# A fused graph network: 92 of 391 edge chunks sorted by source in four classes, ranked in the edge stage, with one-hots shared with ScalarE

## What is computed

```
sums, counts = segment_sum(edge_attr, dst), segment_sum(1, dst)
h0 = concat(x, sums / max(counts, 1), global_feats) @ W.T
x  = layernorm(x + softplus(h0) - log 2)
h  = relu(ln(x @ W1 + b1) * g1 + bt1)
w  = sigmoid(relu(concat(h[src], h[dst]) @ We1 + be1) @ We2 + be2)
aggr = segment_sum(w * h[src], dst)
gate = sigmoid(concat(h, aggr) @ Wg + bg)
x  = layernorm(x + ln(gate * aggr + (1 - gate) * h) * g2 + bt2)
```

## Time and profile before

| | us |
|---|---|
| median of 3 runs (2357.36 to 2359.33) | 2358.75 |
| profiled execution, whole time | 2364.05 |
| its span, first to last instruction | 2362.3 |
| busy in the span: TensorE | 1540.2 |
| VectorE | 1695.0 |
| ScalarE | 582.4 |
| GpSimd | 1452.0 |
| mean granted clock of TensorE | 0.691 of full |

### The profile page before, as it was taken

How to read it: one execution, slowest core, us unless ns; L and a number is a source line. 1 busy time by engine, 2 the same in 40 slices (tenths; PEclk the granted TensorE clock), 3 DMA queues, 4 the chain that set the end, 5 groups by cost and what they waited for, 6 DMA issues and landing times.

```text
span 2362.3 us, 38568 instructions
## 1 busy us (share of the span) xinstructions
PE 1540.2 (65%) x11768; PEld 1351.2 (57%) x11769; DVE 1695.0 (72%) x6954; ACT 582.4 (25%) x1425; POOL 1452.0 (61%) x1465
## 2 busy tenths in 40 slices
PE   5999978973445655665546666667666766665670
PEld 4777867753444544544446666656666655655540
DVE  6666756747988665665557777777778887787767
ACT  0212114640001998888000000000000000000025
POOL 2000001437777777777777777777777777777766
PEclk9999996775555566556556666776767667777675
DMA  7889990145444444444454555555555555555401
GB/s 273 309 304 318 357 345 12 59 150 169 128 132 132 137 135 137 131 130 135 151 163 133 152 157 165 165 163 164 165 159 166 157 168 155 156 163 163 125 22 55
DMA packets 224719, 387.44 MB, mean 164 GB/s; under 512 B 78295, under 2 KB 118264, under 8 KB 224383
## 3 DMA queue, kind: packets, MB, share of 16 engines
q1 hardware_dynamic: 155671, 200.17, 25.7%
q0 software_dynamic: 64704, 176.77, 25.4%
q10 hardware_dynamic: 4136, 8.03, 1.0%
HBM read 369.81 MB, written 15.02 MB: 163 GB/s over the span
## 4 chain that ended last, share of the span: by engine, by line
POOL 38%; PE 27%; issue 19%; DVE 10%; DVEq 2%; DMA 1%; ACT 1%; ACTq 1%; SPq 0%; POOLq 0%
POOL x_rows L717 23%; POOL ring L717 15%; PE bank L402 9%; PE bank L1123 4%; PE bank L449 3%; PE bank L1064 3%; PE bank L409 3%; DVE bank L438 2%; PE bank L429 1%; PE bank L1036 1%; DVEq L1562 1%; DVE sums L1453 1%; PE bank L1015 1%; PE bank L1073 1%; DVE stats L1360 1%
## 5 line engine op out<-in xcount | busy, mean ns | idle before, releaser
L717 POOL DMA_INDIRECT x_rows<-src_table,lane_src x816 | 801.4, 982 | 271.2 <-issue 247.7
L717 POOL DMA_INDIRECT ring<-src_table,lane_src x532 | 522.5, 982 | 162.1 <-issue 161.5
L1138 PE MATMUL bank<-sums 128*128 128x128 f32 x588 | 210.0, 458 | 354.1 <-issue 346.2
L438 DVE SCALAR_TENSOR_TENSOR bank<-bank,we_all 128x128 f32<-128x128 f32 x1642 | 420.5, 324 | 13.0 <-issue 0.4
L1138 PEld LDWEIGHTS bank<-sums 128*128 128x128 f32 x588 | 148.5, 310 | 363.0 <-issue 363.0
L453 DVE TENSOR_TENSOR sums<-sums,bank 128x128 f32 (+1 forms) x728 | 178.2, 245 | 190.3 <-issue 127.5
L686 POOL TENSOR_TENSOR ring<-ring,x_rows 128x512 f32<-128x512 f32 (+1 forms) x13 | 15.7, 1204 | 408.3 <-DVE ring L1350 408.3
L919 ACT ACTIVATE sums<-sums,be_all 128x3 f32<-128x3 f32 x98 | 29.1, 297 | 952.1 <-DVE bank L438 952.1
L449 PE MATMUL bank<-weighted,x_rows 128*128 128x40 f32 x1632 | 254.2, 326 | 2.2 <-DVE sums L453 2.1
L449 PEld LDWEIGHTS bank<-weighted,x_rows 128*128 128x128 f32 x1632 | 253.3, 244 | 2.9 <-issue 2.9
L438 DVE DVE_READ_ACCUMULATOR bank<-bank,we_all 128x1 f32 x1642 | 228.1, 139 | 0.4
(11 more groups left out here) (216 smaller groups left out, 2753.3 us busy)
## 6 DMA issues: line engine op xcount, KB each, us to landing
ring<-in_edge_attr SPq DMA_DIRECT2D x195, 512.0 KB, 5.4
ring<-rel_table SPq DMA_DIRECT2D x84, 512.0 KB, 4.7
x_rows<-src_table,lane_src POOLq DMA_INDIRECT x816
ring<-cell_table SPq DMA_DIRECT2D x33, 384.0 KB, 5.0
ring<-dst_table SPq DMA_DIRECT2D x337, 32.0 KB
ring<-src_table,lane_src POOLq DMA_INDIRECT x532
sums<-src_table SPq DMA_DIRECT2D x49, 128.0 KB, 2.1
src_table<-ring SPq DMA_DIRECT2D x12, 512.0 KB, 3.7
```

Of the source, the lines that this page charges most:

```text
L438: last = eng.scalar_tensor_tensor(hid[:, j, :], hid[:, j, :], 0.0, wide["we2"][:, :], ALU.max, ALU.mult, accum_out=out[:, j:j + 1])
L717: eng.indirect_dma_start(gathered(c)[:, j, :], None, src_table, bass.IndirectOffsetOnAxis(ap=lane_src[:, t:t + 1], axis=0)).then_inc(gathe ...
L1138: eng.matmul(o, src_hot[:, u % 2, k * P:(k + 1) * P], block_rows[:, b % B_SLOTS, 0:P], start=True, stop=False, skip_group_check=True)
```

## The change

The sizes. A class is (first chunk, chunks, cells of 128 for each block). A class has a base row of its own (its first start), so that its destinations lie in 128 nodes from there.

```diff
-SORTED = 54
-CAP = 6
-HALF = CAP // 2
+CLASSES = ((0, 39, 4), (39, 18, 2), (57, 18, 2), (75, 17, 2))
+SORTED = 92
+COLS = 4
...
-    V_SLOTS, G_SLOTS, Q_SLOTS, Q_BATCH = 8, 10, 16, 4
+    V_SLOTS, G_SLOTS, Q_SLOTS, Q_BATCH = 8, 8, 16, 4
...
+        SORT_STEPS = [10] + [3] * (n_classes - 1)
+        SORT_AT = [1]
+        for k in range(1, n_classes):
+            SORT_AT.append(SORT_AT[-1] + sort_len(k - 1) + 5)
...
+        RIDE_AT = CELLS_OUT[0] + 4
+        FOLD_LAG = 2
         def ride(u):
+            return RIDE_AT + u * (n_steps - 1 - FOLD_LAG - RIDE_AT) // (n_riders - 1)
```

**Edge stage.** ScalarE makes the one-hots of pairs 7, 11, ..., 195 (48), three pairs ahead:

```diff
+            def scalar_hot(q):
...
+                for k, c in enumerate(chunks):
+                    for j in range(J):
+                        eng.activation(hots[:, k, j, :], iota1[:, :], ACT.Abs, bias=lane_dst[:, c, j:j + 1], scale=-1.0)
+                eng.drain()
...
+                eng.activation(flat, flat, ACT.Relu, bias=ones[:, 0:1], scale=-1.0).then_inc(done("scalar_hot"), 1)
...
                 eng.activation(pair_rows[0:r, q % 2, :], bank[q % 2][0:r, 0:P], ACT.Copy).then_inc(done("pair_rows"), 1)
+                if q + HOT_PAIRS in scalar_hots:
+                    scalar_hot(q + HOT_PAIRS)
```

On VectorE `hot(q)` does a drain and a semaphore for these pairs, and at set pairs a part of the ranking: `classes_prepared` (pair 3), `couples` (4), a `scan` over 372 for each of 25 couples of blocks (pairs 12 to 14, 30 to 32, ...), `before_`, `check_totals` (166), `kept` (170), `ranked` in five parts (172 to 176). A couple is two blocks; the odd one counts in 2048s. On GpSimd, nine parts of three couples each:

```diff
+            def rank_in(i):
+                n = len(part_couples(i))
+                for k, b in enumerate(part_couples(i)):
+                    eng.tensor_scalar(in_couple[:, i % 2, k, :], couple, float(b), None, ALU.is_equal)
+                eng.drain()
+                eng.tensor_tensor(in_couple[:, i % 2, 0:n, :], in_couple[:, i % 2, 0:n, :],
+                                  parity.unsqueeze(1).to_broadcast([P, n, rank_tokens]), ALU.mult).then_inc(done("rank"), 1)
...
+            def rank_pick(i):
...
+                eng.tensor_tensor(r[:, :, 0:rank_tokens0], r[:, :, 0:rank_tokens0], first_, ALU.add)
+                for k in range(1, n_classes):
...
+                    eng.tensor_tensor(r[:, :, some], r[:, :, some], before[:, i % 2, 0:n, k:k + 1].to_broadcast([P, n, rank_span]), ALU.add)
+                eng.drain()
+                eng.tensor_tensor(r, r, in_couple[:, i % 2, 0:n, :], ALU.mult)
+                for k in range(n):
+                    eng.drain()
+                    last = eng.tensor_tensor(pos[:, :], pos[:, :], r[:, k, :], ALU.add)
```

**Gather stage.** The ranking leaves it. `sort_start` goes to step 0. VectorE's one-hots of the sort carry the value, two a token, and ScalarE makes one column one-hot a token for both (Abs, Relu, width 196 or 98):

```diff
+            def sort_rows(q):
                 for k, t in enumerate(sort_tokens(q)):
+                    for v, value in enumerate((src_low, sorted_dst)):
+                        eng.tensor_scalar(sort_hot(q)[0][:, k, v, :], iota_r, row_of[:, t:t + 1], value[:, t:t + 1], ALU.is_equal, ALU.mult)
```

ScalarE takes over the cell one-hots, the source placement and the copy of the sums; TensorE accumulates in PSUM and folds each rider; the hidden part of a rider has one bank and goes last in TensorE's step:

```diff
             for q in range(n_steps):
                 edge_weight(q)
+                if q - 2 in riders:
+                    sums_out(q - 2)
+                if q in riders:
+                    place_sources(q)
+                if q + 3 in riders:
+                    cell_hots(q + 3)
+                if q + 3 in sort_class:
+                    sort_columns(q + 3)
...
-            run_stages(n_steps, [(1, hidden_mm), (4, wsum)])
+            run_stages(n_steps, [(1, hidden_mm), (4, wsum), (1, rider_mm)])
```

More of the change, by code:

```diff
@@ L680, in residual @@
+            need(eng, "hot", KEYS_AT)
+            rank_in(0)
+            rank_in(1)
+            for i in range(n_parts):
+                rank_totals(i)
+                rank_pick(i)
+                if i + 2 < n_parts:
+                    rank_in(i + 2)
             def residual(g):
@@ new lines, in cell_hots @@
+            def cell_hots(q):
+                u = riders[q]
+                need(eng, "rider_hidden", u - 2)
+                eng.wait_ge(rider_in[u % U_SLOTS], 32 * (u // U_SLOTS + 1))
+                n = rider_cols(u) * P
+                hots = (src_hot[:, u % 2, 0:n], dst_hot[:, u % 2, 0:n])
+                for v, hot_ in enumerate(hots):
+                    eng.activation(hot_, cell_wide[:, u % U_SLOTS, v, 0:n], ACT.Abs, bias=iota_col[:, 0:1])
+                eng.drain()
+                for hot_ in hots:
+                    last = eng.activation(hot_, hot_, ACT.Relu, bias=ones[:, 0:1], scale=-1.0)
+                last.then_inc(done("cell_hot"), 1)
@@ new lines, in place_sources @@
+            def place_sources(q):
+                u = riders[q]
+                need(eng, "wsum", q - 2)
+                n = rider_cols(u)
+                at_ = rider_cells(u).start
+                for i in range(n):
+                    eng.activation(place_src[:, u % 2, i, :], iota_s, ACT.Abs, bias=cell[:, 0, at_ + i:at_ + i + 1], scale=-1.0)
+                eng.drain()
+                hot_ = place_src[:, u % 2, 0:n, :].rearrange("p k n -> p (k n)")
+                eng.activation(hot_, hot_, ACT.Relu, bias=ones[:, 0:1], scale=-1.0).then_inc(done("place_src"), 1)
@@ L1122, in sort_mm @@
+                first = CLASSES[k][0] * J
+                end = first + CLASSES[k][1] * J
+                rows_, cols_ = sort_hot(q)
+                eng.wait_ge(done("col_hot"), sort_order[q] + 1)
+                for i, t in enumerate(sort_tokens(q)):
                     for v in range(2):
-                        eng.matmul(cell_bank(v)[:, 0:cells], row_hot[:, q % 2, k, :], col_hot[q % 2][:, k, v, :],
-                                   start=(t == 0), stop=(t == tokens - 1), skip_group_check=True)
@@ new lines, in scan, with before_ @@
+            def scan(i, k):
+                if k == 0:
+                    eng.wait_ge(done("rank"), rank_done[f"in{i}"])
+                one = in_couple[:, i % 2, k, :]
+                eng.tensor_tensor_scan(running[:, i % 2, k, :], one, one, 0.0, ALU.add, ALU.max)
+            def before_(i):
+                bs = part_couples(i)
+                need(eng, "pair_mm", rank_mm_at(i))
+                eng.tensor_tensor(before[:, i % 2, 0:len(bs), :], rank_out(i).rearrange("p (b k) -> p b k", k=n_classes),
+                                  ends[:, bs[0]:bs[-1] + 1, 0:n_classes], ALU.subtract)
@@ L1410, in _ @@
                 (4, norm1), (1, pre_), (2, soft_sum), (3, moments1_), (NORM2_AT, norm2), (5, moments2_),
[L1411 to L1415 removed]
+                (DST_AT + 1, rest_), (DST_AT + 2, part2), (3, blank)])
+            eng.drain()
+            if columns > padded:
+                step(eng.memset(aggr[:, padded:columns], 0.0))
             def x1_offset(g):
```

711 lines of the change are left out of this document (446 added, 265 removed).

## The result

The changed kernel takes **2211.8 us** (median; 2210.8 to 2215.1) against 2358.1 for the kernel before on the same chip: ratio 0.938, 95% interval 0.937 to 0.940, so 146 us less. The forecast was 2218. In the runs of all experiments but two (out of the lock, and three slot pairs the second time) the kernel before took 2618 to 2664 us and every other kernel more too. Those runs are compared with each other only. The edge variants (beside a kernel before of 2618 or 2626) have a control of the changed kernel; the runs beside 2663.9 have none and are held against each other.

The account below looks back on a forecast made before the run. GpSimd's gather issue was taken to bound the gather stage, TensorE the edge stage. Profiled 2364 - 181 (gather stage) + 40 (edge stage) = 2223, as a median 2218 us; range 2160 to 2310, ends 2130 and 2349.

Parts of the forecast that it names:

- the signs named as wrong: GpSimd waiting for L449 over 30 us, VectorE or TensorE over 95% busy in rider steps, or first gather past 610 us.
- R4: Sorting: a block overflows its cells or a class spans 128 nodes, all 92 chunks go singly, thousands of us; chance 0.01.
- the signs named as right: 1196 gathers in 1540 to 1570 us, stated paces, first gather at 550 to 570, 0.8 us copy idle, one-hots over 1.2.
- the loop: Gather stage, four slots pairs for five: it fits, but queueing takes most of the room; charged 15 us (0 to 60).
- Class 0's steps: Gather stage, steps 1 to 16: VectorE's 20 products a step slow the gathers, 11.1 us a step, 178 us in all.
- Riders' steps: Gather stage: 71 steps with rider and products at 10.25 us, 728 us; 56.5 more, nearly all rider alone, at 10.05, 568.
- ScalarE's one-hots: Edge stage, 48 pairs: 2.9 us each delays the copy, 0.8 us stall in 35 pairs, +28 on TensorE; VectorE saves 33.
- The lock: Edge stage: VectorE's one-hots meeting GpSimd's rank operations lose time, 52 us at most, nothing at least; taken as 30.
- The small operations: Edge stage, VectorE: classes, keys, check, keep and ranks, some 60 operations, +20 us.
- R1: Edge stage hides the ranks (+5 there) and four slots pairs suffice without the 15 us: 2168 us; chance 0.19.
- R2: Gather stage: rider steps leave the gather's pace, 11.0 us with the sort and 10.4 without: 2290 us; chance 0.16.
- R3: Gather stage: TensorE becomes the bound in riders' steps at its low clock, 12.5 and 11.7 us: 2465 us; chance 0.07.

Follow-up runs that it names:

- out of the lock: Changed kernel with split ScalarE one-hots, fourth slot and respaced scans, then GpSimd's part moved two pairs earlier and the check in two pieces: 2202.1 us, ratio 0.932.
- three slot pairs the second time: Changed kernel with three slot pairs for gathered rows instead of four, run beside a kernel before of 2358.4: 2394.0 us, ratio 1.015.
- The edge variants: Changed kernel with ScalarE's one-hots taken back or split, GpSimd's rank work or also scans left out, or rank work respaced: 2442.2 to 2456.6 us.
- the runs beside 2663.9: Changed kernel with three slot pairs 2496.1, last class 11 chunks 2512.4, class 0's products left out 2477.6; kernel before with four slot pairs 2651.9 us.
- the control: The changed kernel once more, unaltered, beside a kernel before of 2626.2: 2455.7 us, ratio 0.936.

## Why the prediction was right, step by step

**What bounds.** Right: the time follows the gathers. None of the signs named as wrong came: GpSimd waited 8.5 us for L542 (30 was the mark), VectorE and TensorE are at 83% and 75% in riders' steps, the first gather came at 557, and with 1196 gathers at their pace no block had overflowed (R4). Of the signs named as right, the 1545 us, the pace of at most 1.30 and the first gather came; the pace of 1.38, the 0.8 us for ScalarE's copy and the slow one-hots "wherever GpSimd adds" didn't (11 of the 56 that met it took over 1.2 us).

**The gather stage**: 1545 us; the sum said 1534, + 15 for the loop, + 4 for the filling, 1553. Three terms were off by 11 to 20 us each and largely cancelled, so that a median of 2211.8 came so near to the 2218 is in part luck; the mechanism and the way are not.
- Class 0's steps were put at 11.1 us and took 10.44, 11 us too much in all; the 10.44 hold the filling already, which the sum charged apart (4), and without the step of 13.7 they are 10.2. The step that failed is "4.7 us of such work gives 1.1". VectorE's work was reckoned right (20 products stand 0.224 us apart, 4.5 us), but its price to GpSimd was carried over from six one-hots (and in proportion, 0.29 x 4.7 / 1.1, it would have been 1.2): the run without them shows about 0.2 us a step. The pace of 1.38 for the first 16 steps was wrong with it.
- Riders' steps were put at 10.25 and 10.05 and took 10.40 and 10.21: 0.15 each, 20 us too little. I had reckoned GpSimd's locked time to be about the same as before; it is longer, and which of the added operations does it no run tells.
- The loop was charged 15 us and cost nothing behind the start. In the changed kernel the first gather of a pair stood on average 8.3 us behind the sums of four pairs back in the riders' steps (5.0 at least). The 7 us of queueing charged against the reckoned "some 7 us" of room weren't there. The 3.65 us at the start are the filling, 4 in the sum. That it *would* bind with a pair fewer the run shows (+182).
- ScalarE's new work: 6.4 us a step for the 7.0 to 8.2, covered. SP's transfers: among riders no engine waited for one of them; the 15.5 us for a window of `dst_table` stand at the stage's start.

**The edge stage**: +37.5 us (+38.9 in the control) for the +40. The sum was right, its parts less so:
- ScalarE's one-hots take 2.80 us (eight of 64 elements 2.01, one of 512 0.72, some overlapping), close to 2.9, but TensorE's pair grows by 0.5 us, not 0.8, in about 30 pairs: 15 us for 28. The Trainium skill's figure ("ScalarE: Activation LUTs", What ACT_TABLE_LOAD costs) gave, as an estimate, a stall of 0.6, nearer than mine (its figures come to 2.63 us for the nine, where the prediction wrote 2.7); for the single activation over 64 it gives 0.33 us, and the trace agrees: 0.337 on average.
- The lock: +19 us on the one-hots, +1 on the scans, for the 30 of VectorE's time; 6 of them on the path. 56 of 146 one-hots met an operation of GpSimd; they took 1.03 us on average and up to 2.78, but 26 of them took under 0.8. Of the 18 that started beside GpSimd's comparison (L822, one input, 1.15 us), 16 took their usual 0.68 to 0.69. The prediction had priced these meetings like the others. The Trainium skill's rule ("SBUF — State Buffer", Who interferes with whom), that the two exclude each other, is what the timelines above show for GpSimd's two-input operations; for its comparison, which reads SBUF too, the trace shows it in the first part alone (last section), and the trace decides. Two thirds of the price stay off the path; that this is VectorE's slack of 0.16 us a pair fits, and no run shows it apart.
- The scans: 0.970 for 0.95; 4.7 us on the path.
- The small operations, +20 of VectorE's time spread over the stage: this was the mis-sized term. 9.4 to 9.9 us come out between pairs 160 and 180 in every variant that keeps them together, as one pair of 3.1 us and five or six of 2.2 to 3.0 (one of 3.7 in the first profile). They are not an average load but bursts against a slack of 0.16 us a pair.
- Not foreseen: the gain side of ScalarE's one-hots. I counted -33 us for VectorE and asked only what ScalarE's queue costs. Taken back, the stage ends 4 us earlier, so that the one-hots on ScalarE bought nothing.

**Node and end stage**: the first -1, within -2 to +5; the second +3.5 where I said untouched. It took 109 to 112 us in all profiles of the changed program and 108 to 109 in the two of the one before; what makes the difference is open.

**The rivals.** R1's second half (four pairs suffice) was right; its first (the edge stage hides the ranks) was not. R2 and R3: no engine reached the gather's pace in the result's runs. R3's reason against held in part: the granted clock rose with the work, 0.66 to 0.73 and 0.78. But its picture, TensorE as the bound in riders' steps, is what the slower runs show, for another cause (the granted clock is 0.74 over the control's profile, not 0.5) and for the kernel before as well.

## What to carry to other kernels

Where one engine issues at a fixed pace, count what it issues and leave the rest; but work moved off it lands in a stage whose engines may have 0.16 us of slack, and there bursts, not sums, set the price. An engine that helps another must be asked where its own queue is waited for: split its help so that the urgent instruction stands behind half of it. Operations of GpSimd and VectorE that exclude each other weren't tamed here by shifting one of them in a stage where both work much of the time; to shorten the long ones would be the next thing to try, which no run here did.

## What the runs showed of the hardware

- Where the kernel before takes 2618 us and more, TensorE's matmuls come one by one for a part of each step, with gaps in which the profile names nothing. A riders' stretch of the control:

```profile
1329.90 0.35 PE L1387 MATMUL bank<-ring,sums 128*128 128x128 f32 x1 [0.88 <-issue]
1331.31 0.22 PE L1389 MATMUL bank<-ring,sums 128*128 128x128 bf16 x1 [1.07 <-issue]
1332.73 0.37 PE L1389 MATMUL bank<-ring,sums 128*128 128x128 bf16 x2 [1.20 <-issue]
1334.17 0.59 PE L1387 MATMUL bank<-ring,sums 128*128 128x128 f32 x2 [1.07 <-issue]
```

  Starts stand 1.41 to 1.44 us apart here, 0.72 elsewhere. TensorE's waits in the gather stage, by line, for the control:

```profile
PE bank L1389 <- issue: 234.8, 322, 1.7
PE bank L1387 <- issue: 162.9, 213, 2.6
```

  398 us, and in the changed kernel's first profile under 1 us on these two lines with "issue" as the cause. GpSimd's waits in the control:

```profile
POOL x_rows L897 <- remote: 182.3, 102, 3.3
POOL ring L897 <- remote: 56.0, 32, 2.1
```

  "Remote" says that the profile finds no instruction near the rise of the semaphore. But the first gather of a pair waits for one semaphore alone, that of the weighted sums of four pairs back, and in the trace it rises 5.6 us (median) behind the modelled end of their last matmul, where the first profile has 0.01. So it is TensorE's delay that GpSimd waits for, 1.84 us ahead of each pair's first gather for 0.33. The step is 11.9 us there for 10.3, and one step of the filling takes 33.1 us for 13.7. The edge stage takes the same time either way. It isn't the chip alone: the record numbers the chip of the runs beside 2663.9 and that of the runs beside 2358.4 alike (14). What TensorE itself waits for stays open.
- A VectorE operation with two inputs from SBUF that starts beside a two-input one of GpSimd ends 0.5 to 0.8 us behind the other's end, whatever its own length: the scan 0.8, the one-hot 0.55 (104.91 for 104.36). Beside GpSimd's comparison (L822, one input) only its first part counts: one-hots that started 0.16 and 0.18 us into it took 0.88 and 0.86, those that started 0.44 us or later the usual 0.68. One of them in the changed kernel; the second comparison runs from about 152.7 to 153.8:

```profile
151.47 2.35 POOL L822 TENSOR_SCALAR x_rows<-x_rows 128x372 bf16<-128x372 f32 x2
...
153.17 0.68 DVE L507 TENSOR_TENSOR ring<-iota,lane_dst 128x512 f32<-128x512 f32 x1
```

  Where VectorE's stood first, GpSimd's two-input operation is the one that grows, 3.01 us for the 2.31 that this product takes otherwise; the last edge variant:

```profile
90.59 0.93 DVE L1578 TENSOR_TENSOR_SCAN x_rows<-x_rows 128x372 f32<-128x372 bf16 x1
90.61 3.01 POOL L846 TENSOR_TENSOR x_rows<-x_rows 128x1116 f32<-128x1116 f32 x1
```
